# Expert products of a routed two-layer network interleaved on TensorE, with the second weight's two f16 parts side by side

## The chip, the cores and the metric

One core of one Trainium2 chip runs the whole kernel. The metric is the device time of one execution in microseconds; the time given for a kernel is the median of its runs. A profiled execution, which has its own time, gives the trace.

## The reference

```
x = x + attn(layernorm(x))       # gated linear recurrence, 32 sequences of 256 tokens, width 128
x = x + ffn(layernorm(x))

def ffn(x):
    h = layernorm(x) * g1 + be1
    x = x + softmax_attention(h) @ Wo             # 16 heads of 8
    m = layernorm(x) * g2 + be2                   # 8192 tokens x 128
    probs = softmax(m @ Wg)                       # 8 experts
    wts, idx = top_k(probs, 2); wts = wts / sum(wts)
    h1 = gelu(m @ W1[e] + b1[e])                  # 128 -> 512, tanh form
    ye = h1 @ W2[e] + b2[e]                       # 512 -> 128
    return x + sum over the two chosen e of wts[e] * ye
```

Only the two chosen experts of each token are computed. The change is in the last four lines, the expert stage.

## The kernel before, in words

The stages run one after another: norm and recurrence, projections, attention in two parts of 16 sequences, each followed by routing (the tokens of each expert are counted, and each token-expert pair gets a row in the DRAM buffer `expert_in`). Then comes the expert stage, then a gather of the two result rows of every token from `expert_out`, and the weighted sum.

**The expert stage** works on 80 blocks (`NBLK`) of 256 rows (`BS`), 40 for each part of the tokens. A block belongs to one expert, whose number stands in the table `blke`; each engine loads it into a register (`value_load`) and uses it to address the weights. Numbers are carried as two f16 parts, high and low, and a product is the sum of three: high by high, high by low, low by high. For each block:

- **Load** (SyncE, `load_block`, L439): a DMA that transposes the block's 256 rows of f16 pairs into `XT[q]`, one of four buffers, and raises `xt_in[q]`.
- **up** (TensorE): for each of four chunks of 128 hidden units, three products over 256 columns, 12 in all, into the PSUM banks 2 to 5. It waits for `xt_in` and for the gelu of two blocks before, which frees the banks.
- **gelu** (ScalarE, L834): four activations of 128x256 from PSUM to `G32` (two buffers), with the bias.
- **split** (VectorE): L1145 makes the high part `GH` in f16, L1147 the low part `GL`. Each has two buffers; a split waits until the down product two blocks before is done.
- **down** (TensorE): for each half of 128 rows and each of four chunks, three products over 128 columns, 24 in all, into bank 6 or 7. The gelu parts are the stationary operand, the weight parts `w2h`, `w2l` the moving one.
- **y_out** (VectorE, L1153): adds the bias of the expert (`b2s`, spread over all partitions) to the 128x256 result and writes `YB`; then `yb_ready` rises.
- **Store** (SyncE, `store_block`, L435): `YB` to `expert_out`.

All TensorE products are recorded on line L1191, that of the helper `mm`.

**The order** is set by each engine's program; `blocks` runs the first four blocks and the last eight straight, and those between in a loop with four blocks in its body. In iteration b TensorE does up(b+2), then down(b). VectorE does split(b+1), then y_out(b-1). ScalarE is two blocks ahead. SyncE's order is `blocks_io`: in iteration b it waits for `up_done` of block b (whose `XT` buffer the load takes), issues the load of block b+4, then waits for `yb_ready` of block b and issues its store. A load of block b+4 therefore stands in SyncE's queue behind the store of block b-1.

GpSimd scatters the rows of the second part into `expert_in` during the first 30 blocks (L620, paced by `down_done`), and gathers rows of the first part during the last 40 (L662, paced by `down_done` too); 64 gathers of the second part follow when all stores are done. During attention it splits the expert weights in `split_weight`; before the second sequence's `expand` it has nothing else of the expert stage.

```
for b in range(first, 4): body(b, b % 4)
with eng.Fori(r0, r1) as r:
    for q in range(4): body(4 * r + q, q)
for b in range(NBLK - 8, NBLK): body(b, b % 4)
```

Of the kernel before, what the change touches and what calls it, by code (L numbers as in the profile page):

```python
# [6 lines left out]
ALU = mybir.AluOpType  # L7
# [56 lines left out]
def layer_kernel(nc, x, w_hg, b_hg, w_out, b_out, h0, g1, be1, g2, be2, wq, wk, wv, wo, wg, w1, b1,  # L64
# [8 lines left out]
    with ctx:  # L73
        def sb(name, shape, dt=F32):
            return ctx.enter_context(nc.sbuf_tensor(name, shape, dt))

        def sem(name):
            return ctx.enter_context(nc.semaphore(name))
# [35 lines left out]
        wos = sb("wos", [P, D])  # L114
        wgs = sb("wgs", [P, NE])
        b1s = sb("b1s", [P, NE * FC])
        b2s = sb("b2s", [P, NE, D])
        wst = [sb(f"wst{s}", [P, F]) for s in range(2)]
        w1h, w1l, w2h, w2l = (sb(n, [P, NE, F], F16) for n in ("w1h", "w1l", "w2h", "w2l"))
# [33 lines left out]
        CN = view(2 * D).rearrange("p (t d) -> p t d", t=2)  # L153
        CNT = view(SL)

        at[0] = 0
        MT = [view(2 * 512) for _ in range(2)]

# [15 lines left out]
        GH = [view(FC * BS, F16) for _ in range(2)]  # L174
        GL = [view(FC * BS, F16) for _ in range(2)]
        YB = [view(2 * D).rearrange("p (h d) -> p h d", h=2) for _ in range(2)]

        at[0] = 0
# [8 lines left out]
        bout_in = sem("bout_in")  # L187
        params_in = sem("params_in")
        more_in = sem("more_in")
        x_in = [sem(f"x_in{k}") for k in range(NO)]  # L190
        dve_own = sem("dve_own")
        pool_own = sem("pool_own")
# [143 lines left out]
        def _(sp):  # L336
# [10 lines left out]
            def more(dst, src):  # L347
                sp.dma_start(dst, src).then_inc(more_in, 16)
# [23 lines left out]
            par(wgs[:, :], wg)  # L372
            more(blkn[:, :], const_blk)
            more(b1s[:, :], b1)
            more(b2s[:, :, :], b2.rearrange("(a e) d -> a e d", a=1).broadcast_to([P, NE, D]))

            sp.wait_ge(x_in[NO - 1], 16)
            sp.wait_ge(zero_ready, 1)
# [82 lines left out]
        def _(pool):  # L461
# [116 lines left out]
                    last.then_inc(va_ready, 1)  # L578

            def split_weight(k):  # L580
                whi, wlo = (w1h, w1l) if k < NE else (w2h, w2l)
                e, src = k % NE, wst[k % 2][:, :]
                pool.wait_ge(wst_in[k % 2], 16 * (k // 2 + 1))
# [4 lines left out]
                nc.gpsimd.tensor_copy(whi[:, e, :], src).then_inc(wsplit, 1)  # L588
                pool.wait_ge(wsplit, 2 * k + 1)
                nc.gpsimd.tensor_tensor(wlo[:, e, :], src, whi[:, e, :], ALU.subtract).then_inc(wsplit, 1)  # L590

            pool.wait_ge(rows_clear, 16 * (NBLK * BS // 512))
            expand(0)
            expand(1)
            for b in range(2, SEQ0[1]):
                expand(b)
                split_weight(b - 2)
# [249 lines left out]
        def _(dve):  # L847
# [159 lines left out]

            def b1_add(k):
                dve.wait_ge(b1_done, k + 1)
                dve.wait_ge(more_in, 48)  # L1010
# [61 lines left out]
            def route(part):  # L1072
# [12 lines left out]
                dve.wait_ge(more_in, 48)  # L1085
# [53 lines left out]

            def split(b, s):
                dve.wait_ge(gelu_done, b + 1)
                used(dve, down_done, b - 1)
                V.tensor_copy(GH[s], G32[s]).then_inc(gh_own, 1)  # L1145
                dve.wait_ge(gh_own, b + 1)
                V.tensor_tensor(GL[s], G32[s], GH[s], ALU.subtract).then_inc(gl_ready, 1)  # L1147

            def y_out(b, s):
                e = dve.value_load(blke[0:1, bass.ds(b, 1)], min_val=0, max_val=NE - 1)  # L1150
                dve.wait_ge(down_done, b + 1)
                used(dve, yb_out[s], 8 * (b - s))
                V.tensor_tensor(YB[s], bank[6 + s][:, 0:2 * D].rearrange("p (h d) -> p h d", d=D),  # L1153
                                b2s[:, bass.ds(e, 1), :].broadcast_to([P, 2, D]), ALU.add).then_inc(yb_ready, 1)

            def experts(b, q):
                if exists(b + 1):
                    split(b + 1, (q + 1) % 2)
                if exists(b - 1):
                    y_out(b - 1, (q + 1) % 2)  # L1160

            blocks(dve, -1, experts)
            y_out(NBLK - 1, 1)

# [23 lines left out]
        def _(pe):  # L1189
# [262 lines left out]
            pe.wait_ge(tab_ready, 2)  # L1452
            pe.wait_ge(wsplit, 4 * NE)

            def expert_of(b):
                return pe.value_load(blke[0:1, bass.ds(b, 1)], min_val=0, max_val=NE - 1)

            def part(w, e, c):
                return w[:, bass.ds(e, 1), P * c:P * c + P].rearrange("p a f -> p (a f)")

            def up(b, q):
                s = q % 2
                e = expert_of(b)
                pe.wait_ge(xt_in[q], 4 * (b - q) + 16)
                used(pe, gelu_done, b - 1)
                for c in range(FC):
                    dst = bank[2 + 2 * s + c // 2][:, BS * (c % 2):BS * (c % 2) + BS]
                    mm(dst, part(w1h, e, c), XT[q][:, 0, :], stop=False)
                    mm(dst, part(w1h, e, c), XT[q][:, 1, :], start=False, stop=False)
                    last = mm(dst, part(w1l, e, c), XT[q][:, 0, :], start=False)  # L1470
                last.then_inc(up_done, 1)

            def down(b, s):
                e = expert_of(b)
                pe.wait_ge(gl_ready, b + 1)
                used(pe, yb_ready, b - 1)
                for h in range(2):
                    dst = bank[6 + s][:, P * h:P * h + P]
# [5 lines left out]
                last.then_inc(down_done, 1)  # L1484

            def experts(b, q):
                if exists(b + 2):
                    up(b + 2, (q + 2) % 4)
                if exists(b):
                    down(b, q % 2)  # L1490

            blocks(pe, -2, experts)

# [38 lines left out]
```

## Time and profile before

| | us |
|---|---|
| median of three runs | 1227.25 |
| lowest, highest | 1223.43, 1246.7 |
| the profiled execution | 1236.04 |
| its span | 1234.2 |
| expert stage, first up product to last store's issue | 824.9 to 1139.6 |
| what follows (gathers, weighted sum, output) | 1139.6 to 1234.2 |
| TensorE, VectorE, ScalarE, GpSimd busy, whole span | 852.9, 834.6, 605.0, 471.1 |

Of the 1.84 us between the profiled time and its span nothing stands in the trace. Times in the trace count from the start of the span. An engine's row says when an instruction began and how long it took. "issue" means that the engine waited for nothing that the profile shows, which is the case when its own sequencer had not yet handed it the next instruction. A chain row says what the end of the kernel hung on at that time.

### The profile page before, as it was taken

All of it is one profiled execution on the core that took longest, in us unless ns stands there. A gap on an engine that the chain in (4) does not pass through costs nothing.

```text
span 1234.2 us, 27025 instructions
## 1 busy us (share of the span) xinstructions
PE 852.9 (69%) x8846; PEld 516.5 (42%) x8847; DVE 834.6 (68%) x1670; ACT 605.0 (49%) x1225; POOL 471.1 (38%) x548
## 2 busy tenths in 40 slices
PE   2577476688888884578888887448888888888000
PEld 1355344134443332513333333436666666666000
DVE  6778687768778846688888881845555555556622
ACT  3545288157677774227777775414444443333000
POOL 5800296002212123413333332735554045544774
PEclk9989799569999997559999997559999999999555
DMA  6900024211111110001111110013333233333422
GB/s 162 360 2 1 1 103 154 69 37 53 44 45 53 53 58 1 0 18 49 52 55 47 47 36 14 1 39 88 97 97 94 68 94 96 96 95 93 134 70 68
DMA packets 132213, 84.70 MB, mean 69 GB/s; under 512 B 54534, under 2 KB 117642, under 8 KB 132122
## 3 DMA queue, kind: packets, MB, share of 16 engines
q1 hardware_dynamic: 123930, 66.71, 18.7%
q0 software_dynamic: 8192, 16.79, 4.9%
q8 instruction: 55, 0.90, 0.3%
q14 instruction: 36, 0.29, 0.1%
HBM read 30.77 MB, written 41.94 MB: 59 GB/s over the span
## 4 chain that ended last, share of the span: by engine, by line
PE 52%; DVE 25%; issue 9%; POOL 7%; ACT 3%; DMA 2%; another core or an unknown queue 2%; DVEq 0%; SPq 0%; ACTq 0%; POOLq 0%
PE bank L1191 49%; DVE arena L1004 9%; POOL rr L466 2%; DVE arena L1147 2%; DVE mom L861 2%; DVE arena L940 2%; POOL Z L662 2%; POOL xh L470 2%; POOL HT L662 1%; DVE arena L1145 1%; PE bank L1371 1%; PE bank L1378 1%; DMA arena<-expert_in 1%; PE bank L1195 1%
## 5 line engine op out<-in xcount | busy, mean ns | idle before, releaser
L1004 DVE TENSOR_REDUCE arena<-bank 128x2 f32<-128x512 f32 x512 | 337.2, 688 | 85.0 <-PE bank L1191 82.9
L754 ACT ACTIVATE arena<-bank 128x512 f32<-128x512 f32 x512 | 292.8, 596 | 136.0 <-PE bank L1191 133.0
L1191 PE MATMUL bank<-QK 32*128 32x256 f16 (+1 forms) x2048 | 206.9, 288 | 91.3 <-DVE arena L1004 68.0
L620 POOL DMA_INDIRECT expert_in<-HT,idx x128 | 134.5, 1051 | 253.8 <-PE bank L1191 226.3
L834 ACT ACTIVATE arena<-bank,b1s 128x256 f32<-128x256 f32 x320 | 125.5, 476 | 179.6 <-PE bank L1191 120.1
L1191 PEld LDWEIGHTS bank<-QK 31*128 31x128 f16 (+1 forms) x2048 | 63.5, 93 | 241.6 <-ACT arena L754 177.6
L1191 PE MATMUL bank<-w2h,arena 128*128 x1280 | 143.0, 221 | 24.7 <-issue 15.7
L1191 PE MATMUL bank<-arena,VA 128*32 128x256 f32 x2048 | 145.7, 405 | 1.4 <-ACT arena L754 1.4
L1145 DVE CAST arena<-arena 128x1024 f16<-128x1024 f32 x80 | 55.5, 694 | 131.9 <-PE bank L1191 121.1
L1191 PE MATMUL bank<-arena,w1h 128*128 128x256 f16 x640 | 112.1, 277 | 33.9 <-issue 21.4
L1191 PEld LDWEIGHTS bank<-w2h,arena 128*128 128x128 f16 x1280 | 110.2, 96 | 52.1 <-issue 46.7
L1191 PE MATMUL bank<-w2l,arena 128*128 x640 | 122.7, 217 | 0.0
L1195 PE MATMUL bank<-cst,xh 128*128 128x128 f32 x192 | 44.9, 387 | 86.0 <-ACT xh L793 32.6
L662 POOL DMA_INDIRECT Z<-expert_out,idx x64 | 68.9, 1076 | 89.6 <-DMA expert_out<-arena 48.1
L466 POOL TENSOR_TENSOR rr<-vv,mhalf 128x8 f32<-128x8 f32 (+1 forms) x24 | 49.8, 2074 | 133.3 <-DVE vv L878 132.0
L1147 DVE TENSOR_TENSOR arena<-arena 128x1024 f16<-128x1024 f32 x80 | 98.1, 1226 | 2.7
L1191 PE MATMUL bank<-arena,w1l 128*128 128x256 f16 x320 | 88.4, 276 | 0.0
L662 POOL DMA_INDIRECT HT<-expert_out,idx x64 | 68.1, 1063 | 44.7 <-PE bank L1191 27.0
L1191 PEld LDWEIGHTS bank<-arena,w1h 128*128 x640 | 56.0, 99 | 54.5 <-issue 47.3
L1191 PEld LDWEIGHTS bank<-arena,VA 128*32 128x32 f32 x2048 | 55.2, 113 | 55.0 <-issue 25.2
L1195 PEld LDWEIGHTS bank<-cst,xh 128*128 128x128 f32 x192 | 31.3, 198 | 95.6 <-issue 49.5
L1191 PEld LDWEIGHTS bank<-w2l,arena 128*128 128x128 f16 x640 | 61.8, 96 | 0.8 <-issue 0.2
(148 smaller groups left out, 1213.5 us busy)
## 6 DMA issues: line engine op xcount, KB each, us to landing
QK<-qk_parts SPq DMA_DIRECT2D x96, 128.0 KB
expert_in<-arena SPq DMA_DIRECT2D x40, 256.0 KB, 3.6
expert_out<-arena SPq DMA_DIRECT2D x80, 128.0 KB
qk_parts<-arena SPq DMA_DIRECT2D x16, 512.0 KB, 2.8
X<-x SPq DMA_DIRECT2D x8, 512.0 KB, 5.9
wst<-w SPq DMA_DIRECT2D x16, 256.0 KB, 2.8
out<-arena SPq DMA_DIRECT2D x16, 256.0 KB
expert_in<-HT,idx POOLq DMA_INDIRECT x128, 2.2
```

Source lines behind the costliest of these rows:

```text
L466: nc.gpsimd.tensor_tensor(rr[j % 2][:, 0:n, :], vv[j % 2][:, 0:n, :], mhalf[:, 0:n, :], ALU.pow)\
L470: return nc.gpsimd.tensor_scalar(dst, src, rr[j % 2][:, n, t:t + 1], nmr[j % 2][:, n, t:t + 1], ALU.mult, ALU.add)
L620: pool.indirect_dma_start(xs, bass.IndirectOffsetOnAxis(idx[:, k, n:n + 1], 0), MHL[:, n, :], None).then_inc(scattered[n // HN], 16)
L662: pool.indirect_dma_start(gat[k][:, n, :], None, ys[0:BS * BLK0[part + 1], :], bass.IndirectOffsetOnAxis(idx[:, k, n:n + 1], 0))\
L754: nc.scalar.activation(PT[t % 8], bank[2 + t % 2][:, :], ACT.Exp, scale=DH ** -0.5)\
L834: last = nc.scalar.activation(G32[s][:, BS * c:BS * c + BS], bank[2 + 2 * s + c // 2][:, BS * (c % 2):BS * (c % 2) + BS], ACT.Gelu_apprx_t ...
L861: last = V.bn_stats(mom[:, t, :], buf[:, 8 * j + t, :])
L1004: V.tensor_reduce(nmax[n % 2][:, :, 4 * j + g], bank[u % 2][:, :].rearrange("p (q t) -> p q t", q=2), AX.X, ALU.max, negate=True).then_inc ...
L1145: V.tensor_copy(GH[s], G32[s]).then_inc(gh_own, 1)
L1147: V.tensor_tensor(GL[s], G32[s], GH[s], ALU.subtract).then_inc(gl_ready, 1)
L1191: return nc.tensor.matmul(dst, lhsT, rhs, start=start, stop=stop)
L1195: last = nc.tensor.transpose(bk[:, P * t:P * t + P], src[:, t0 + t, :], ident)
```

## The change

- TensorE: in iteration b it does up(b+3) and down(b), and their products alternate in the program: one of up, then one or two of down, twelve turns. All four waits (`xt_in`, `gelu_done`, `gl_ready`, `yb_ready`) stand ahead of the first product. The expert numbers are kept where they can be: seven loads of a number for four blocks in place of eight.
- down: the two parts of the second weight lie side by side in `w2p`, so that the high gelu part meets both in one product of 256 columns; the low gelu part meets the high weight in one of 128 columns. The output bias is one more product for each half, of `ones16` with `b2h`, whose rows 0 and 32 hold its two f16 parts. That is 8 products of 256 columns and 10 of 128 in place of 24 of 128. The result takes a whole bank, two partial sums side by side.
- VectorE: y_out becomes a reduction over the two partial sums (512 elements in, 256 out of each partition) and loads no expert number; in iteration b it does y_out(b-1) first, then split(b+2). `GH` and `GL` have four buffers, in the memory of `QK`.
- SyncE's order is as it was. The broadcast load of `b2s` (512 KB) becomes two loads of 4 KB. GpSimd makes `b2h` between expand(1) and expand(2): a memset, two copies and a subtraction.

```
 def split_weight(k):
-    whi, wlo = (w1h, w1l) if k < NE else (w2h, w2l)
+    if k < NE: whi, wlo = w1h[:, e, :], w1l[:, e, :]
+    else: ... whi, wlo = w2p[:, e, :, 0, :], w2p[:, e, :, 1, :]
...
+nc.gpsimd.memset(b2h[:, :, :], 0.0).then_inc(b2_own, 1)
+pool.wait_ge(more_in, 64)
+pool.wait_ge(b2_own, 1)
+for r in (0, 32):
+    nc.gpsimd.tensor_copy(b2h[r:r + 1, :, :], b2in[r:r + 1, :, :]).then_inc(b2_own, 1)
+pool.wait_ge(b2_own, 3)
+nc.gpsimd.tensor_tensor(b2h[32:33, :, :], b2in[32:33, :, :], b2h[32:33, :, :], ALU.subtract)
...
-def split(b, s):
+def split(b, q):
     dve.wait_ge(gelu_done, b + 1)
-    used(dve, down_done, b - 1)
+    used(dve, down_done, b - 3)
...
 def y_out(b, s):
-    e = dve.value_load(blke[0:1, bass.ds(b, 1)], min_val=0, max_val=NE - 1)
     dve.wait_ge(down_done, b + 1)
     used(dve, yb_out[s], 8 * (b - s))
-    V.tensor_tensor(YB[s], bank[6 + s][:, 0:2 * D]..., b2s[:, bass.ds(e, 1), :].broadcast_to([P, 2, D]), ALU.add)
+    V.tensor_reduce(YB[s], bank[6 + s][:, :].rearrange("p (h k d) -> p h d k", h=2, k=2), AX.X, ALU.add)
...
 def experts(b, q):                       # VectorE
-    if exists(b + 1): split(b + 1, (q + 1) % 2)
     if exists(b - 1): y_out(b - 1, (q + 1) % 2)
+    if exists(b + 2): split(b + 2, (q + 2) % 4)
...
 def down(b, q, e):                       # TensorE, a generator now, as up is
     for h in range(2):
         for c in range(FC):
-            mm(dst, GH[s][:, x], part(w2h, e, c), start=c == 0, stop=False)
-            mm(dst, GH[s][:, x], part(w2l, e, c), start=False, stop=False)
-            last = mm(dst, GL[s][:, x], part(w2h, e, c), start=False, stop=c == FC - 1)
+            w = w2p[:, bass.ds(e, 1), c, :, :].rearrange("p a k d -> p (a k d)")
+            mm(dst, GH[q][:, x], w, start=c == 0, stop=False)
+            yield
+            w = w2p[:, bass.ds(e, 1), c, 0, :].rearrange("p a d -> p (a d)")
+            mm(dst[:, 0:P], GL[q][:, x], w, start=False, stop=False)
+            yield
+        last = mm(dst[:, P:2 * P], ones16[:, :], b2h[:, bass.ds(e, 1), :]..., start=False)
...
 def experts(b, q):                       # TensorE
-    if exists(b + 2): up(b + 2, (q + 2) % 4)
-    if exists(b): down(b, q % 2)
+    u, qu = b + 3, (q + 3) % 4
+    if q == 0: known.clear()
+    for x, k in ((u, q + 3), (b, q)):
+        if exists(x) and k not in known: known[k] = expert_of(x)
+    if exists(u):
+        pe.wait_ge(xt_in[qu], 4 * (u - qu) + 16)
+        used(pe, gelu_done, u - 1)
+        ups = up(u, qu, known[q + 3])
+    if exists(b):
+        pe.wait_ge(gl_ready, b + 1)
+        used(pe, yb_ready, b - 1)
+        downs = down(b, q, known[q])
+    for turn in range(12):
+        for _ in zip(range(1), ups): pass
+        for _ in zip(range(1 + turn % 2), downs): pass
```

## Rows read from the trace of the kernel before

**Rows 1.** Engines by stretch: start:end, length, busy (instructions), granted clock, DMA share, GB/s.
```profile
220.00:260.00 40.00, 31.57 (x192) 8.41 (x196) 28.84 (x45) 12.65 (x22) 0.00 (x0) 0.50 0.16 46
...
844.00:884.00 40.00, 33.31 (x368) 26.66 (x366) 22.67 (x31) 15.70 (x40) 21.95 (x20) 1.00 0.39 100
```

**Rows 2.** Groups of instructions by form, 844 to 1130 us.
```profile
L1191 PE MATMUL bank<-w2h,arena 128*128 x1175 | 131.2, 221 | 22.4 <-issue 14.7 <-DVE arena L1147 6.2 <-DVE arena L1153 1.5
L834 ACT ACTIVATE arena<-bank,b1s 128x256 f32<-128x256 f32 x295 | 115.8, 475 | 171.9 <-PE bank L1191 113.2 <-issue 43.0 <-DVE arena L1147 15.7
...
L1191 PE MATMUL bank<-arena,w1h 128*128 128x256 f16 x592 | 101.6, 274 | 24.2 <-issue 21.4 <-DMA arena<-expert_in 1.2
...
L1147 DVE TENSOR_TENSOR arena<-arena 128x1024 f16<-128x1024 f32 x74 | 90.7, 1226 | 2.5
...
L1145 DVE CAST arena<-arena 128x1024 f16<-128x1024 f32 x73 | 50.7, 694 | 117.3 <-PE bank L1191 117.3
```

**Rows 3.** The chain that ended last, in order of time, expert stage: start, us, what.
```profile
822.01 2.71 DMA arena<-expert_in
824.93 2.75 PE bank L1191 x12
...
843.78 1.48 PE bank L1191 x12
...
904.52 1.79 PE bank L1191 x24
906.39 1.48 PE bank L1191 x12
...
1127.42 1.48 PE bank L1191 x12
```

**Rows 4.** Timeline of TensorE within one down product, both halves.
```profile
904.63 0.22 PE L1191 MATMUL bank<-w2l,arena 128*128 x1
...
904.87 0.22 PE L1191 MATMUL bank<-w2l,arena 128*128 x1
...
905.53 0.22 PE L1191 MATMUL bank<-w2l,arena 128*128 x1
...
905.70 0.22 PE L1191 MATMUL bank<-w2l,arena 128*128 x1
```

**Rows 5.** TensorE's sequencer, loads of an expert number: ns min/median/max, first and last start.
```profile
L1456 PEldq TENSOR_LOAD <-blke x147: 296/303/631, 844.7 to 1128.4; - x147
```

**Rows 6.** The chain that ended last, unmerged, 1108 to 1145 us.
```profile
1115.08 0.43 DVE arena L1153
...
1116.27 3.76 DMA arena<-expert_in
...
1120.16 1.48 PE bank L1191 x12
...
1137.18 1.87 PE bank L1191 x24
...
1139.18 0.43 DVE arena L1153
```

**Rows 7.** Timeline of SyncE's queue, blocks in the steady stretch.
```profile
893.30 0.38 SPq L435 DMA_DIRECT2D expert_out<-arena  x1
893.81 1.20 SPq L439 DMA_TRANSPOSE arena<-expert_in  x1
896.90 0.38 SPq L435 DMA_DIRECT2D expert_out<-arena  x1
897.91 1.20 SPq L439 DMA_TRANSPOSE arena<-expert_in  x1
```

**Rows 8.** Costliest groups of the page: a reduction of 512 PSUM elements on VectorE.
```profile
L1004 DVE TENSOR_REDUCE arena<-bank 128x2 f32<-128x512 f32 x512 | 337.2, 688 | 85.0 <-PE bank L1191 82.9
```

**Rows 9.** Timeline of GpSimd in attention, idle time in brackets.
```profile
261.63 0.53 POOL L576 COPY VA<-HT 128x128 f32<-128x128 f32 x2 [53.33 <-PE bank L1191]
```

More of the change, by code:

```diff
@@ L116, in layer_kernel @@
         b1s = sb("b1s", [P, NE * FC])
-        b2s = sb("b2s", [P, NE, D])
+        b2h = sb("b2h", [P, NE, D], F16)
         wst = [sb(f"wst{s}", [P, F]) for s in range(2)]
-        w1h, w1l, w2h, w2l = (sb(n, [P, NE, F], F16) for n in ("w1h", "w1l", "w2h", "w2l"))
+        w1h, w1l = (sb(n, [P, NE, F], F16) for n in ("w1h", "w1l"))
+        w2p = sb("w2p", [P, NE, FC, 2, D], F16)
         QK = [sb(f"QK{s}", [P, 4, 2, SL], F16) for s in range(4)]
@@ L154, in layer_kernel @@
         CNT = view(SL)
+        at[0] = 5472
+        b2in = view(NE * D).rearrange("p (e d) -> p e d", d=D)
         at[0] = 0
@@ L173, in layer_kernel @@
         G32 = [view(FC * BS) for _ in range(2)]
-        GH = [view(FC * BS, F16) for _ in range(2)]
-        GL = [view(FC * BS, F16) for _ in range(2)]
+        GH, GL = ([QK[s][:, 2 * k:2 * k + 2, :, :].rearrange("p a b t -> p (a b t)") for s in range(4)]
+                  for k in range(2))
         YB = [view(2 * D).rearrange("p (h d) -> p h d", h=2) for _ in range(2)]
@@ L580, in split_weight @@
             def split_weight(k):
-                whi, wlo = (w1h, w1l) if k < NE else (w2h, w2l)
                 e, src = k % NE, wst[k % 2][:, :]
+                if k < NE:
+                    whi, wlo = w1h[:, e, :], w1l[:, e, :]
+                else:
+                    src = src.rearrange("p (c d) -> p c d", d=D)
+                    whi, wlo = w2p[:, e, :, 0, :], w2p[:, e, :, 1, :]
                 pool.wait_ge(wst_in[k % 2], 16 * (k // 2 + 1))
@@ L1453, in _, with up_part, up @@
             pe.wait_ge(wsplit, 4 * NE)
+            pe.wait_ge(b2_ready, 1)
             def expert_of(b):
                 return pe.value_load(blke[0:1, bass.ds(b, 1)], min_val=0, max_val=NE - 1)
-            def part(w, e, c):
+            def up_part(w, e, c):
                 return w[:, bass.ds(e, 1), P * c:P * c + P].rearrange("p a f -> p (a f)")
[L1461 to L1465, printed above, removed]
-                for c in range(FC):
[L1467 to L1470, printed above, removed]
+            def up(b, q, e):
+                for c in range(FC):
+                    dst = bank[2 + 2 * (q % 2) + c // 2][:, BS * (c % 2):BS * (c % 2) + BS]
+                    mm(dst, up_part(w1h, e, c), XT[q][:, 0, :], stop=False)
+                    yield
+                    mm(dst, up_part(w1h, e, c), XT[q][:, 1, :], start=False, stop=False)
+                    yield
+                    last = mm(dst, up_part(w1l, e, c), XT[q][:, 0, :], start=False)
+                    if c < FC - 1:
+                        yield
@@ L1471, in up, with down @@
                 last.then_inc(up_done, 1)
[L1473 to L1476, printed above, removed]
+                yield
+            def down(b, q, e):
                 for h in range(2):
-                    dst = bank[6 + s][:, P * h:P * h + P]
+                    dst = bank[6 + q % 2][:, 2 * P * h:2 * P * h + 2 * P]
                     for c in range(FC):
                         x = slice(BS * c + P * h, BS * c + P * h + P)
-                        mm(dst, GH[s][:, x], part(w2h, e, c), start=c == 0, stop=False)
-                        mm(dst, GH[s][:, x], part(w2l, e, c), start=False, stop=False)
-                        last = mm(dst, GL[s][:, x], part(w2h, e, c), start=False, stop=c == FC - 1)
+                        w = w2p[:, bass.ds(e, 1), c, :, :].rearrange("p a k d -> p (a k d)")
+                        mm(dst, GH[q][:, x], w, start=c == 0, stop=False)
+                        yield
+                        w = w2p[:, bass.ds(e, 1), c, 0, :].rearrange("p a d -> p (a d)")
+                        mm(dst[:, 0:P], GL[q][:, x], w, start=False, stop=False)
+                        yield
+                    last = mm(dst[:, P:2 * P], ones16[:, :], b2h[:, bass.ds(e, 1), :].rearrange("p a d -> p (a d)"),
+                              start=False)
+                    if h == 0:
+                        yield
@@ L1484, in down @@
                 last.then_inc(down_done, 1)
+                yield
+            known = {}
             def experts(b, q):
-                if exists(b + 2):
-                    up(b + 2, (q + 2) % 4)
-                if exists(b):
-                    down(b, q % 2)
-            blocks(pe, -2, experts)
+                u, qu = b + 3, (q + 3) % 4
+                if q == 0:
+                    known.clear()
+                for x, k in ((u, q + 3), (b, q)):
+                    if exists(x) and k not in known:
+                        known[k] = expert_of(x)
+                ups, downs = [], []
+                if exists(u):
+                    pe.wait_ge(xt_in[qu], 4 * (u - qu) + 16)
+                    used(pe, gelu_done, u - 1)
+                    ups = up(u, qu, known[q + 3])
+                if exists(b):
+                    pe.wait_ge(gl_ready, b + 1)
+                    used(pe, yb_ready, b - 1)
+                    downs = down(b, q, known[q])
+                for turn in range(12):
+                    for _ in zip(range(1), ups):
+                        pass
+                    for _ in zip(range(1 + turn % 2), downs):
+                        pass
@@ L1496 @@
+            blocks(pe, -3, experts)
 def kernel(**inputs):
```

29 lines of the change are left out of this document (17 added, 12 removed).

## The prediction

>
> Inside a period an up product takes 1.48 us for 12 instructions [rows 3]; the last needs 0.27 of it (274 ns, rows 2), so one starts every 0.11. In a down product three start in 0.24 us in the first half and in 0.17 in the second [rows 4]: 0.080 and 0.057 each. Both halves have the same shapes. What differs is that the second uses weight addresses that the first has already worked out. So where addresses are new the sequencer sets the pace: 12 products with 8 addresses take 0.96 us, 0.12 for an address. Starts sum to 12 x 0.11 + 12 x 0.080 + 12 x 0.057 = 2.96 us; the other 0.87 of the period are the gaps ahead of up and down, where the sequencer loads an expert number (0.30 us median, up to 0.63 [rows 5], plus the arithmetic around it; I take 0.7 in all) and waits for semaphores. The bound now is TensorE's sequencer, serial: two numbers, 16 addresses, four waits.
>
> **TensorE's own work after.** Products: 12 + 8 of 256 columns, 8 + 2 of 128. By the starts above 20 x 0.11 + 10 x 0.057 = 2.77 us against 12 x 0.11 + 24 x 0.057 = 2.69 at the same pace, so the array has 0.08 us more to do. From first start to last end it is 2.77 - 0.06 + 0.22 = 2.93, which I call M. The sequencer loses three addresses (8 for up, 4 for down, 1 for the bias, if both slices of `w2p` at chunk c, which begin at one address, share it) and a quarter of a number: 3.83 - 0.36 - 0.17 = 3.30 us. The pure gain of interleaving would therefore be 0.5 us a block, 39 us over 74. That is what I don't expect to see, because of the next part.
>
> **The load of XT comes onto the path.** Up now runs three blocks ahead, but SyncE's order is unchanged. The load of block b+4 is queued behind the store of b-1, which waits for y_out(b-1), which waits for the end of down(b-1). Before, up(b+4) stood in iteration b+2, two periods (7.7 us) after that end. Now it stands in iteration b+1, and its wait stands ahead of all 30 products, so down(b+1) waits too. The loop: start of iteration b-1, M, y_out, store issue, load, start of iteration b+1. That is 2P = M + L. L, step by step:
> - end of down to start of y_out: 1139.05 to 1139.18, 0.13 [rows 6].
> - y_out: 128x512 from PSUM. The nearest row is another reduction of 512 PSUM elements, 0.69 us [rows 8]. It writes 2 elements, this one 256. Below it can't be less than the 0.43 of the present y_out [rows 6]; above I put twice the row, 1.38. I take 0.69.
> - end of y_out to issue of the load: 1115.51 to 1116.27, 0.76 [rows 6]. In the steady stretch the load follows the start of the store by 0.51 us, and by 1.01 once in four, where the loop wraps [rows 7]. Over four it is some 0.70, and 0.17 before the store gives 0.87. Ends: 0.70 and 1.2.
> - issue to landing: 2.71 with nothing else moving [rows 3], 3.76 beside gathers [rows 6]. No row shows a plain one in the middle; a scatter runs beside it there. I take 2.6, near the lower row, for bounds of 2.2 and 3.76.
> - landing to first product: 1120.03 to 1120.16, 0.13 [rows 6], and two more waits behind `xt_in` (for the split and for y_out), which before stood elsewhere, at an estimated 0.1 each: 0.33.
>
> L = 0.13 + 0.69 + 0.87 + 2.6 + 0.33 = 4.62, and P = (2.93 + 4.62) / 2 = 3.78. The blocks of one parity carry the wrap and the pair goes by the slower, so 3.80.
>
> **The other loops.** VectorE does split(b+3) between y_out(b) and y_out(b+1). Up(b+3) ends 2.7 us into iteration b, gelu takes up to 4 x 0.475 = 1.9, the split 0.69 + 1.23 [rows 2], hand-overs 0.2: done at 6.7. Y_out(b+1) is due at P + M + 0.13 = 6.86. So it is in time with 0.1 to spare, and as a loop over three periods (6.7 + 0.69 + 0.87 + 2.6 + 0.33 = 11.2) it asks for 3.73 only. VectorE's work is 0.69 + 1.23 + 0.69 = 2.6 of 3.80. ScalarE's is unchanged. Four `GH` and `GL` buffers remove a wait that cost little.
>
> **Start and tail.** The first blocks hang on gelu(0) to (2) and the stores as before; up(5) still needs the load behind the store of block 0, so I take no gain there. After up(79) begins, the old kernel needed 12.2 us to the last store (1127.42 to 1139.6). The new one has M = 2.9 with down(76), three downs at 1.45 of products and 0.5 of gap, and y_out 0.8: 9.6, say 10. Gain 2.2. The gathers behind the last store are untouched.
>
> **GpSimd's bias preparation** falls into 53.3 us of idle time ahead of the third `expand` [rows 9]; four instructions, the larger of 1024 elements on one partition, an estimated 6 us at most. Nothing, and 6 us if that cover were gone. The smaller bias DMA ends long before its first use: nothing either way.
>
> **Sum.** 74 x (3.83 - 3.80) = 2.2, and 2.2 of the tail: 4.4 us less than the profiled 1236.04, so 1231.6. The shown median is 1227.25, 0.7% below the profiled one; at the same ratio the changed kernel comes to 1222.8. I forecast 1222.
>
> **Two rules weighed.** Rows 4 show down products starting 0.057 us apart, each with a new 128-column stationary operand. The Trainium skill (TensorE: Matmul & The Clock Gate, "LDWEIGHTS (loading the stationary operand)") gives a load the operand's columns over 1.2, an estimated 107 ns here; taken as serial work that would be 36 x 0.107 = 3.85 us before and 30 x 0.107 = 3.21 after, 46 us faster. By that rule; the trace disagrees, since 24 such products took 1.79 us [rows 3].
>
> The first of rows 1 is a stretch ahead of the steady part of attention, with TensorE busy 31.6 of 40 us at a granted clock of 0.50, the 1.2 GHz level. So a busy engine alone does not guarantee the clock, and after the change the array stands still some 0.9 us in 3.8, for a transfer. The same page of the Trainium skill ("Loop structure matters more than you think") calls a DMA wait between groups of products bad for the clock. By that rule the change would be slower; in the trace the old loop has 0.87 us of gaps at 1.00.
>
> **The rivals.**
> - *Faster, the load is cheaper than I think.* With 2.2 for the landing, 0.70 for SyncE and 0.25 after it, 2P = 2.93 + 0.13 + 0.69 + 0.70 + 2.2 + 0.25 = 6.90, P = 3.45: 28 + 2 us less, 1197. For it: the DMA engines are busy only 0.39 of the time [rows 1]. Against: both landings in the rows are above 2.7.
> - *Slower, the same loop at its upper prices.* The alternating reduction at 1.1 and the landing at 3.2, as beside gathers: 2P = 8.56, P = 4.28: 33 - 2 us more, 1258. The loop decides for slower from 2P = 7.73 on, for slower by 2% from 8.4. For it: the 3.76 row, and gathers run beside the second 40 blocks. Against: only a few loads show it.
> - *Addresses not shared* (17 instead of 13). The sequencer needs 3.78, and the first half of the products is paced by it, M = 3.13: P = 3.90, 5 - 2 us more, 1230.
> - *The clock falls.* Twelve up products took 2.75 at the low clock against 1.48 [rows 3]; M doubles to 5.8, P = 5.2, some 100 us more, 1327.
> - *Weight loads bound* as by the page: 1181.
>
> **Chances.** Forecast 0.60, cheaper load 0.13, dearer load 0.13, addresses 0.09, clock 0.03, weight loads 0.02. A measurement of this kernel tells about 2% from no change. Faster: 0.13 + 0.02 = 0.15; slower: 0.13 + 0.03 = 0.16; the rest, 0.69, within. The forecast's own spread (landing 2.4 to 2.9) is 1212 to 1236; the range runs toward the two load cases, 1197 to 1250.
>
> **What the profile would show.** TensorE's idle time put down to the load of `arena` from `expert_in` or to "issue" right behind it, some 0.8 us once per block; 30 products as one run of 2.9 us; y_out at 0.69, its store and then the load about 0.9 behind its end; the period 3.80. It is wrong if TensorE waits for nothing and the period is near 3.4, if the wait is for the split, or if y_out takes over 1 us.

## The result and the profile after

The changed kernel took 1232.9 us against 1226.1 (medians of 18 runs each); the ratio is 1.0047, 95% interval 1.0025 to 1.0070. The forecast was 1222. Two later comparisons of the same kernel gave 0.9995 (0.9967 to 1.0023) and 1.0029 (1.0003 to 1.0055), so it is even or a few tenths of a per cent slower, and not faster by the 0.4% of the forecast. The profiled execution took 1232.73 us, span 1230.9. All ratios leave out the executions that took over 1.5% more than the fastest of their kernel; where such a long one is the profiled one, as with two blocks behind, its extra time lies ahead of the expert stage.

Who waited for whom, changed kernel, 850 to 1130 us (engine, line, releaser: us in total, times, longest):

```profile
DVE QK L1165 <- ACT arena L854: 57.3, 71, 1.0
PE bank L1209 <- DMA arena<-expert_in: 55.1, 58, 2.2
...
PE bank L1209 <- ACT arena L854: 12.6, 7, 2.0
```

TensorE's wait for the load of `XT` was 1.2 us before, in the row of the up products [rows 2]. It is 55.1 now, at 58 places, and the "issue" that stood beside it in rows 2 (14.7 and 21.4 us) is no longer among TensorE's waits. VectorE's split waited 117.3 us behind TensorE [rows 2] and now waits 57.3 for the gelu. The last row, TensorE behind the gelu, belongs to the load as well. The program asks there only for the gelu of up(b+1), which ended long before. At the first block of a loop body the products begin 0.45 us after the load has landed, and where a later gelu ends within that time the row names it: products begin at 911.63 us, their load landed at 911.18, a gelu ended at 911.51. Each of the seven has its load landed 0.13 to 0.50 us ahead. The chain says the same where it passes through the load, and carries the loop link by link. The chain that ended last, changed kernel:

```profile
836.55 2.94 PE bank L1209 x30
...
958.08 2.95 PE bank L1209 x30
...
961.14 0.70 DVE arena L1172
...
962.61 2.65 DMA arena<-expert_in
...
965.40 2.94 PE bank L1209 x30
...
1131.80 2.95 PE bank L1209 x30
```

Thirty products in 2.95 us, 0.11 to the reduction, 0.70 for it, 0.77 to the issue of the load (962.61 less 961.84), 2.65 to its landing, 0.14 to the next 30: 7.32 us. Those next 30 are two iterations on, since the iteration between hangs on the load before. This loop is one of the short ones. The mean of the 56 between 870 and 1090 us is 7.77, which is 3.88 a block. SyncE's queue in the changed kernel (L442 is the store, L446 the load):

```profile
899.72 0.38 SPq L442 DMA_DIRECT2D expert_out<-arena  x1
...
900.31 1.20 SPq L446 DMA_TRANSPOSE arena<-expert_in  x1
...
910.84 0.38 SPq L442 DMA_DIRECT2D expert_out<-arena  x1
911.86 1.20 SPq L446 DMA_TRANSPOSE arena<-expert_in  x1
```

The load follows the start of the store by 0.59 us, and by 1.02 where the loop wraps; it was 0.51 and 1.01 before [rows 7].

For the period, the first and last y_out of a stretch and their count serve best. The row of y_out in the changed kernel and in the kernel before, 870 to 1096 us (ns min/median/max, first and last start):

```profile
L1172 DVE TENSOR_REDUCE arena<-bank x58: 680/691/693, 871.2 to 1093.1; 128x256 f32<-128x512 f32 x58
```

```profile
L1153 DVE TENSOR_TENSOR arena<-bank,b2s x58: 416/417/418, 873.3 to 1095.2; 128x256 f32<-128x256 f32 x58
```

Both are 221.9 us over 57 steps, 3.893 us a block. This part of the stage did not move at all. In these two profiles the difference lies outside it. Stretches of the changed kernel (length, busy TensorE, weight loads, VectorE, ScalarE, GpSimd, granted clock, DMA share, GB/s); the two of 3.4 us were chosen after the clock's own record:

```profile
844.00:884.00 40.00, 29.39 (x271) 24.62 (x271) 22.95 (x27) 13.67 (x36) 17.24 (x18) 0.91 0.33 88
884.00:924.00 40.00, 30.50 (x313) 26.23 (x314) 26.07 (x32) 16.72 (x43) 19.04 (x20) 1.00 0.37 97
...
1084.00:1120.00 36.00, 27.37 (x252) 22.87 (x250) 20.96 (x25) 12.56 (x32) 13.34 (x13) 0.91 0.35 87
...
846.80:850.20 3.40, 3.40 (x22) 2.59 (x20) 0.00 (x0) 0.06 (x1) 0.00 (x0) 0.51 0.00 0
...
1116.50:1119.90 3.40, 3.40 (x21) 2.62 (x19) 0.64 (x1) 0.00 (x0) 0.00 (x0) 0.50 0.17 38
```

In four spells (from 846.8, 863.9, 1099.4 and 1116.5) the clock was granted at 0.50, the 1.2 GHz level, with TensorE busy throughout and 22 products in such a stretch. Some 1 us before each spell a standstill of 2.0 us or more had ended. Two of these waits, timeline of TensorE, idle time in brackets:

```profile
845.71 0.28 PE L1209 MATMUL bank<-arena,w1h 128*128 128x256 f16 x1 [2.85 <-DMA arena<-expert_in]
...
1098.32 0.28 PE L1209 MATMUL bank<-arena,w1h 128*128 128x256 f16 x1 [2.21 <-DMA arena<-expert_in]
```

TensorE in the kernel before never stood for 1.6 us in this stage once down had begun. The sum of the stage, after against before: first product to up(5) 15.7 against 18.8 us (-3.2); up(5) to up(79) 295.25 against 287.23 (+8.0, the spells' part); up(79) to the last store 10.2 against 8.6 (+1.6). Together that is +6.4 us. It is close to the 6.8 us between the medians, but it doesn't explain them: of these two profiled executions the changed kernel's is the shorter one, by 3.3 us, since what lies outside the stage was 9.7 us shorter in it. Nor do the first and second term stay the same from one profile to the next, as the table at the end of the experiments shows.

### The profile page after: what moved, and what is told of

Read it like the earlier page. It is cut to its first block, busy times and chain, and to the rows that moved or that the text cites. A ratio compares the mean times of both kernels' runs of the same rounds, so it can differ in the third digit from the quotient of the medians.

```text
span 1230.9 us, 25465 instructions
## 1 busy us (share of the span) xinstructions
PE 826.3 (67%) x8366; PEld 510.8 (41%) x8367; DVE 860.6 (70%) x1669; ACT 604.6 (49%) x1225; POOL 453.4 (37%) x552
## 4 chain that ended last, share of the span: by engine, by line
PE 44%; DVE 23%; POOL 9%; DMA 9%; issue 8%; ACT 4%; SPq 1%; ACTq 0%; DVEq 0%; POOLq 0%
PE bank L1209 41%; DVE arena L1024 9%; DMA arena<-expert_in 8%; POOL Z L682 2%; POOL HT L682 2%; POOL rr L473 2%; DVE arena L1172 2%; DVE mom L881 2%; POOL xh L477 2%; DVE arena L960 2%; PE bank L1389 1%; SPq L442 1%; ACT arena L854 1%; PE bank L1396 1%; PE bank L1213 1%
## 5 line engine op out<-in xcount | busy, mean ns | idle before, releaser
L1209 PE MATMUL bank<-arena,w1h 128*128 128x256 f16 x640 | 170.9, 282 | 84.0 <-DMA arena<-expert_in 68.6
L640 POOL DMA_INDIRECT expert_in<-HT,idx x128 | 124.8, 975 | 266.7 <-PE bank L1209 239.2
L1209 PE MATMUL bank<-w2p,QK 128*128 x1280 | 221.6, 250 | 1.6 <-DVE arena L1172 1.6
L1209 PEld LDWEIGHTS bank<-w2p,QK 128*128 128x128 f16 x1280 | 126.0, 99 | 14.2 <-issue 1.7
L1209 PEld LDWEIGHTS bank<-arena,w1h 128*128 x640 | 64.2, 101 | 103.1 <-issue 96.8
L1165 DVE CAST QK<-arena 128x1024 f16<-128x1024 f32 x80 | 55.6, 696 | 70.4 <-ACT arena L854 70.4
L1167 DVE TENSOR_TENSOR QK<-arena,QK 128x1024 f16<-128x1024 f32 x80 | 98.0, 1226 | 2.7
L682 POOL DMA_INDIRECT Z<-expert_out,idx x64 | 61.9, 967 | 100.7 <-PE bank L1209 82.5
L1172 DVE TENSOR_REDUCE arena<-bank 128x256 f32<-128x512 f32 x80 | 55.0, 689 | 44.1 <-PE bank L1209 42.2
L583 POOL COPY VA<-HT 128x128 f32<-128x128 f32 x64 | 16.8, 297 | 100.9 <-PE bank L1209 100.9
```

The lines of the kernel that those rows point to most:

```text
L640: pool.indirect_dma_start(xs, bass.IndirectOffsetOnAxis(idx[:, k, n:n + 1], 0), MHL[:, n, :], None).then_inc(scattered[n // HN], 16)
L682: pool.indirect_dma_start(gat[k][:, n, :], None, ys[0:BS * BLK0[part + 1], :], bass.IndirectOffsetOnAxis(idx[:, k, n:n + 1], 0))\
L1165: V.tensor_copy(GH[q], G32[q % 2]).then_inc(gh_own, 1)
L1167: V.tensor_tensor(GL[q], G32[q % 2], GH[q], ALU.subtract).then_inc(gl_ready, 1)
L1172: V.tensor_reduce(YB[s], bank[6 + s][:, :].rearrange("p (h k d) -> p h d k", h=2, k=2), AX.X, ALU.add) .then_inc(yb_ready, 1)
L1209: return nc.tensor.matmul(dst, lhsT, rhs, start=start, stop=stop)
```

## The experiments

Each comparison is with the kernel before, run on the same chip; ratios carry a 95% interval. The period is worked out as above from the row of y_out, over 870 to 1080 us.

**Load issued ahead.** The changed kernel with SyncE's order altered (block 4's load is issued ahead of the loop, after the first up product):

```
-                if exists(b + 4):
-                    sp.wait_ge(up_done, b + 1)
-                    load_block(b + 4, q)
+                if exists(b + 5):
+                    sp.wait_ge(up_done, b + 2)
+                    load_block(b + 5, (q + 1) % 4)
                 store_block(b, q % 2)
```

> The changed kernel with one edit on SyncE: the load of block b+5 is issued ahead of the store of block b, so a load no longer stands behind the store of the block before last. Theory (the load of XT came onto the path; behind it the sequencer of TensorE, 3.30 us a block, or gelu and split set the pace): TensorE's wait for that load goes, the period falls from 3.99 to 3.3 to 3.5 us, the granted clock stays at 1.00 in the expert stage, and the time is 1185 to 1205. Rival (products alternating, or the reduction on VectorE, make the block slow, and the load is only what ends last): at most 5 us less, 1228 to 1233.

Measured 0.9693 (0.9654 to 0.9733), 1202.9 us on a chip where the kernel before took 1236.9. Rows of the up products and of y_out, this run:

```profile
L1211 PE MATMUL bank<-arena,w1h 128*128 128x256 f16 x496 | 130.0, 273 | 31.5 <-DVE QK L1169 24.6 <-issue 6.9
```

```profile
L1174 DVE TENSOR_REDUCE arena<-bank x62: 683/689/693, 871.4 to 1079.2; 128x256 f32<-128x512 f32 x62
```

The wait for the load is gone, a wait for the split (L1169) has taken a part of its place, and the period is 207.8 / 61 = 3.41. (The 3.99 of the expectation is 295.25 / 74, with the spells in it.) Moving one load in SyncE's program is worth 3.5% here: the load was the bound.

**The same order in the kernel before.**

> The kernel before with the same edit on SyncE. Theory: it has two periods for a load and its own sequencer bounds it, so nothing moves: 1222 to 1230. Rival (loads queued behind stores cost time there too): 5 to 30 us less.

Measured 0.998 (0.995 to 1.001), period 3.89. Nothing moved, so the old kernel has no load on its path, and the change put it there.

**Two blocks behind instead of three**, products alternating.

```
-                u, qu = b + 3, (q + 3) % 4
+                u, qu = b + 2, (q + 2) % 4
```

> The changed kernel with down two blocks behind up instead of three (products alternating all the same, VectorE splits block b+1 in iteration b, six numbers loaded for four blocks, SyncE as it was). Theory: the load has a period more and leaves the path; next is the loop up, gelu, split, down over two blocks, about 6.8 us, so 3.4 a block: 1185 to 1200. Rival (alternating products are slow themselves): 1228 or more. Rival (split on the path costs more than three blocks of distance would): 3.8 or more a block, 1222 and above.

Measured 0.9767 (0.9734 to 0.9801), period 3.57. The load has left the path. The chain of this run shows what took it over:

```profile
934.58 2.88 PE bank L1209 x28
...
938.74 0.49 ACT arena L854
939.34 0.69 DVE QK L1165
940.07 1.24 DVE QK L1167
...
941.65 2.93 PE bank L1209 x30
```

From one run of products over gelu and split to the next but one, 7.07 us for two blocks. The loop was foreseen at 6.8: the place was right, and the price 0.3 us too low.

**The new shape alone**, in the old order and not alternating:

```
+            def experts(b, q):
+                if exists(b + 2):
+                    e = expert_of(b + 2)
+                    ...
+                    for _ in up(b + 2, (q + 2) % 4, e): pass
+                if exists(b):
+                    e = expert_of(b)
+                    ...
+                    for _ in down(b, q, e): pass
```

> The kernel before in its order (up two ahead, then down, not alternating; eight numbers for four blocks), with the second weight's parts side by side, the bias by TensorE and the reduction on VectorE. Theory (the sequencer bounds the block; three addresses of 0.12 us go): 3.83 - 0.36 = 3.47 us a block, 1196 to 1206. Rival (the array bounds it, and has 0.08 us a block more to do): 1230 to 1234.

Measured 0.9724 (0.9662 to 0.9787), 1201.95 us. y_out in this run:

```profile
L1172 DVE TENSOR_REDUCE arena<-bank x61: 683/684/685, 871.8 to 1079.3; 128x256 f32<-128x512 f32 x61
```

```profile
L1209 PEldq FUSED_REGOPS  x549: 46/46/46, 870.4 to 1079.5; - x183
...
L1209 PEldq ALU_OP  x244: 32/32/36, 870.5 to 1078.1; - x122
```

That is 793 in 61 blocks, 13 a block. The kernel before has 432 and 432 in 54 blocks, 16 a block, and the changed kernel 13 again.

**Four addresses put back.** On that kernel, `w2p[..., c, 0, :]` for the low gelu part becomes `w2p[..., c, 1, :]`: this leaves out the product of the low gelu part with the high weight and makes one with the low weight instead, of the same shape, from another address.

> The kernel of the run with the new shape alone, but the low gelu part meets the low half of the second weight instead of the high one, so that part of the product is another number than the reference's; the shapes and counts are the same, but each chunk has two weight addresses instead of one, four more for a block. Theory (0.12 us of sequencer for an address): 0.48 us a block more, 3.9, so 33 to 38 us above that run, a ratio of 0.995 to 1.005 to the kernel before. Rival (addresses are hidden behind products): under 8 us more.

Measured 1.008 (1.005 to 1.011).

```profile
L1172 DVE TENSOR_REDUCE arena<-bank x52: 676/684/684, 872.9 to 1078.7; 128x256 f32<-128x512 f32 x52
```

205.8 / 51 = 4.04: 0.58 us for four addresses, 0.144 each, the same price from the other side. The count of register instructions is 889 in 52 blocks, 17 a block.

**Fewer numbers.** The new shape alone, with the number of up(b+2) kept for down where both stand in one body of the loop (`known[q + 2] = expert_of(b + 2)`).

> The kernel of the run with the new shape alone (up two ahead, not alternating), and the number of an expert loaded for up is kept for down where both stand in one loop body: six loads of a number for four blocks in place of eight. Theory (TensorE's sequencer sets the period, a number costs it 0.7 us): half a load a block less, 0.35 us of 3.45, so some 24 us less than that run, a ratio of 0.95 to 0.96 to the kernel before, unless the loop of gelu and split (about 3.3 a block) ends the gain at half. Rival (the array or VectorE sets the period there): no change, 0.97.

Measured 0.9629 (0.9577 to 0.968), 1185.95 us, period 206.8 / 63 = 3.28. A gain of 0.18, half of the 0.35 of half a number. The expectation had that figure as its second case, but with another cause: TensorE's waits for gelu and split come to 4.8 us between 870 and 1090 us, and its up products waited 8.9 us for loads.

**Both.** That kernel with the load issued ahead.

> The fastest kernel so far (new shape, products not alternating, six numbers for four blocks) with the load of block b+5 ahead of the store of block b. Theory: its own profile still shows a little waiting for loads, some 9 us in the steady 220 us; most of that goes, 3 to 8 us less, a ratio of 0.956 to 0.961 to the kernel before. Rival (the loop of gelu and split takes it over): no change, 0.963.

Measured 0.9597 (0.9527 to 0.9668), 1174.65 us: the fastest of all, ahead of both kernels by 4%.

```profile
L1174 DVE TENSOR_REDUCE arena<-bank x67: 682/683/685, 870.7 to 1079.3; 128x256 f32<-128x512 f32 x67
```

Period 208.6 / 66 = 3.16. The intervals of this run and the one before overlap; the step between them is not settled by the times, but the period fell by 0.12.

**The fastest kernel, alternating.** Two behind, six numbers, load ahead, products alternating and all waits ahead of them. VectorE's order differs too: it sums before it splits.

> The fastest kernel (two behind, six numbers, load ahead) with its products alternating and all waits ahead of them, as in the changed kernel; VectorE sums before it splits. Theory: alternating gives the sequencer nothing it did not have, and now up waits for the split of the block that down needs: the loop up, gelu, split, down of two blocks stays at 3.5 us a block, as in the run two behind: a ratio of 0.970 to 0.980 to the kernel before, some 20 us slower than the fastest. Rival (alternating hides addresses and numbers behind longer products): 3.19 or less, 0.96 or less.

Measured 0.9851 (0.9803 to 0.9899), period 208.9 / 59 = 3.54, against 3.16 without alternating. It is slower than expected by 0.005, but on the side of the theory. Between 870 and 1080 us TensorE waited 13.6 us for the split and 12.3 us for y_out, ahead of up products that need neither. What alternating, the place of the waits and VectorE's order cost by themselves was not separated. The period is also that of the run with two blocks behind (3.57), which has the old order of loads: there the load had indeed left the path.

**A dearer step in the loop, first.** Each store as two DMAs of 128 rows.

> The changed kernel with each store issued as two DMAs of 128 rows instead of one of 256, so that the load behind it is issued about 0.45 us later. Theory (period is half of M + L): 0.22 us a block more, some 17 us more than the changed kernel, a ratio of 1.015 to 1.022 to the kernel before, more if the clock falls oftener. Rival (the load is not on the path): no change, 1.005. Rival (the wait is one period long, not two): 0.45 a block, 33 us, 1.03.

Measured 1.0107 (1.0074 to 1.014), below the expected 1.015 to 1.022. SyncE's queue and then the chain of this run:

```profile
899.69 0.86 SPq L443 DMA_DIRECT2D expert_out<-arena  x2
900.79 1.20 SPq L446 DMA_TRANSPOSE arena<-expert_in  x1
```

```profile
897.00 2.67 DMA arena<-expert_in
899.80 2.94 PE bank L1209 x30
902.76 0.70 DVE arena L1172
904.82 2.69 DMA arena<-expert_in
907.64 2.94 PE bank L1209 x30
```

The load is issued 1.10 us after the start of the store instead of 0.59, and this loop is 7.84 us from one run of products to the next but one.

**The second, on VectorE.** The reduction done twice, first into an unused tile.

```
+                V.tensor_reduce(YD[s], bank[6 + s][:, :].rearrange("p (h k d) -> p h d k", h=2, k=2), AX.X, ALU.add)
                 V.tensor_reduce(YB[s], bank[6 + s][:, :].rearrange("p (h k d) -> p h d k", h=2, k=2), AX.X, ALU.add)
```

> The changed kernel with each reduction of VectorE done twice, first into an unused tile: 0.73 us more between the end of down and the store. Theory (the period is half of M + L): 0.36 us a block more, 27 us, a ratio of 1.024 to 1.030 to the kernel before, and the split stays beside it, since VectorE is then at 3.3 us a block. Rival (the load is not on the path): 1.005. Rival (the wait returns every block): 0.73 a block, 54 us, 1.049.

Measured 1.0184 (1.0112 to 1.0255), below the expected 1.024 to 1.030.

Between 1041 and 1080 us this profile has four spells at half the clock, and the run before has one at 1040.2. So the period is compared ahead of them. Rows of y_out, 870 to 1035 us, in the changed kernel, with the store in two and with the reduction twice:

```profile
L1172 DVE TENSOR_REDUCE arena<-bank x43: 680/691/693, 871.2 to 1033.7; 128x256 f32<-128x512 f32 x43
```

```profile
L1172 DVE TENSOR_REDUCE arena<-bank x42: 684/692/693, 871.0 to 1034.0; 128x256 f32<-128x512 f32 x42
```

```profile
L1174 DVE TENSOR_REDUCE arena<-bank x41: 678/680/682, 872.3 to 1032.1; 128x256 f32<-128x512 f32 x41
```

The periods are 3.87, 3.98 and 4.00. From the end of down to the issue of the load the two runs take 0.47 and 0.59 us more than the changed kernel, in the mean of the loops that begin between 870 and 1030 us, and the block grew by 0.11 and 0.13. Both runs reject a price of nothing and one that returns every block. Half of what was added, the price by M + L, is 0.23 and 0.30, and they fall short of that too: in the same loops the landing and the step from it to the products are together 0.29 and 0.32 us shorter than in the changed kernel. With that the loops add up, as the parts of a loop must; it is no test of the theory, and why the landing is shorter is not known. It isn't that slower loops have shorter landings. The medians of the loads issued between 870 and 1090 us, read from the events of their semaphores, are 2.57 us in the kernel before (period 3.89), 2.90, 2.75 and 2.60 in the three profiles of the changed kernel, 2.57 with its load ahead (3.41), and 2.81 in the fastest kernel (3.16). In the third profile of the changed kernel a quarter of the landings is not recorded.

**The changed kernel again, and fillers.** Eight products of 128 columns into an unused bank ahead of the waits. Four runs: fillers, the kernel as it is, and then both side by side on one chip.

```
+                if exists(u) and exists(b):
+                    for _ in range(8):
+                        mm(bank[0][:, 0:P], ones16[:, :], ones16[:, :])
```

> The changed kernel with eight products of 128 columns into an unused bank ahead of the waits of each iteration, 0.46 us of array work inside the 0.5 to 1.3 us in which TensorE waits for the load. Theory (four spells at half the clock in the expert stage cost the profiled run about 7 us, and the load loop alone comes out even with the kernel before): the granted clock stays at 1.00 there, the period is 3.89, and the time is 4 to 8 us less than the changed kernel's, a ratio of 0.997 to 1.001 to the kernel before. Rival (the 6 us come from the loop itself): the ratio stays at 1.005 or rises, since the shorter gaps grow.

> The changed kernel as it is, beside the run with the doubled reduction and on the same chip. Theory: in the expert stage the granted clock falls again for a few short spells, not at the same blocks, since the stage stands still for the load each block; ratio to the kernel before 1.002 to 1.008. Rival (the four spells of the first profile were chance): 1.00 throughout and a ratio of 1.000.

> The changed kernel as it is, on the same chip and beside the run with fillers that follows. Theory (spells at half the clock are what puts it above the kernel before): its ratio lies above that of the run with fillers by 0.002 to 0.005, and runs with a lower mean clock are the longer ones. Rival (spells make no difference that can be measured): the two ratios agree within 0.001.

> The changed kernel with eight filler products ahead of the waits, again, beside the changed kernel. Theory: no or one spell at half the clock in the expert stage, and a ratio of 0.997 to 1.000 to the kernel before. Rival (fillers lengthen the short gaps as much as they save): the ratio is at or above the changed kernel's.

Fillers gave 1.0005 (0.9979 to 1.0031) and 0.9992 (0.9969 to 1.0014); the kernel as it is 0.9995 (0.9967 to 1.0023) and 1.0029 (1.0003 to 1.0055). So the second comparison of the kernel as it is met its rival, no spell and a ratio of 1.000, and not the theory; and fillers did not keep every spell away, the first run with them has one (a granted clock of 0.96 between 844 and 884 us). Side by side the difference is 0.0037, as the theory has it, but the intervals overlap. In the changed kernel the executions with a lower mean clock are indeed the longer ones, by some 9 us for 0.01 of clock, but so are those of the kernel before, by some 8, though its profile has no spell in this stage. So that part of the expectation came true without telling for the spells. Stretches of the second profile of the kernel as it is, and of the side-by-side pair (without and with fillers):

```profile
844.00:884.00 40.00, 28.07 (x290) 24.03 (x288) 24.82 (x30) 15.70 (x40) 17.60 (x19) 1.00 0.37 91
...
1084.00:1120.00 36.00, 28.12 (x292) 24.22 (x289) 24.59 (x29) 14.40 (x37) 16.36 (x16) 1.00 0.39 99
```

```profile
884.00:1084.00 200.00, 152.15 (x1547) 130.46 (x1547) 132.68 (x156) 80.87 (x207) 71.88 (x74) 0.99 0.35 91
```

```profile
884.00:1084.00 200.00, 178.83 (x1975) 153.80 (x1975) 133.93 (x157) 81.21 (x209) 71.27 (x75) 1.00 0.36 92
```

The expert stage in seven profiles (us; a spell is a stretch at half the clock, counted after the first 20 us):

| | first product to up(5) | up(5) to up(79) | up(79) to last store | spells |
|---|---|---|---|---|
| kernel before | 18.8 | 287.2 | 8.6 | 0 |
| kernel before, load ahead | 17.4 | 287.4 | 8.6 | 0 |
| changed kernel | 15.7 | 295.3 | 10.2 | 4 |
| changed kernel, second | 15.8 | 287.0 | 10.2 | 0 |
| changed kernel, third | 18.4 | 288.3 | 10.1 | 1 |
| with fillers | 15.7 | 290.0 | 10.1 | 1 |
| with fillers, second | 18.1 | 287.2 | 10.1 | 0 |

In the profile without a spell up(5) to up(79) took 286.96 us, where the one with four needed 295.25: 8.3 us, some 2 for each spell. That is shown, and that the rest of the loop is even with the kernel before. The last column but one is 1.5 us longer in every profile of the changed kernel. The first column differs as much between executions of one kernel as between the kernels. That spells make up what the first comparison has above 1.000 is possible and not shown, since times and spells were recorded together in only five executions.

## Why the prediction was wrong

- **The bound before** was named rightly: the sequencer, with its addresses and numbers. An address was put at 0.12 us; two runs measured 0.144 and 0.145 in the period.
- **One row was read wrongly.** The up product at 1127.42 is up(78), not up(79); the last stands inside the next chain row and began at 1131.01. Over 74 blocks the period before was 287.23 / 74 = 3.88, not 3.83, and the old tail 8.6 us, not 12.2. The two errors cancel in the sum, but they hid that the new tail, 10.2 us (10 was forecast), is longer than the old one.
- **The load comes onto the path:** right, with 2P = M + L. Means of the 56 loops that begin between 870 and 1090 us: M was put at 2.93 and is 2.93; end of down to the reduction 0.13 and 0.13; the reduction 0.69 and 0.69; SyncE 0.87 and 0.86; landing to first product 0.33 and 0.26 (0.13 in half of them, 0.45 at the first block of each loop body).
- **The step that failed** is the landing in L, "issue to landing: I take 2.6". It is 2.90 in the mean and in the median of these loops. So L is 4.84 and not 4.62, and P = (2.93 + 4.84) / 2 = 3.88 and not 3.78. Against the true base the forecast of 3.80 would have been a gain of 0.08 us in each of 74 blocks, 6 us; the measured period in the steady part is that of before. In the second profile the landing is 2.82 in the mean and the loop 7.72; in the third the loop is 7.78, with a spell in it and its landings recorded in part. The choice was near what the same load took in the kernel before, 2.57 in the median, which stood in no row. The forecast's own spread, 1212 to 1236, has the landing at up to 2.9, so the size was allowed for and the wrong value chosen. Why it lands later in the changed kernel stays open.
- **The tail** was the other half of the forecast gain and has the wrong sign: 2.2 us were to be won, and 1.5 were lost in every profile.
- **The clock** was a rival with all or nothing: half speed in every block, 100 us, 0.03. What came is in between: a few spells, four in the first profile, 8 us. The page of the Trainium skill that warns of a long wait for a DMA ahead of products (TensorE: Matmul & The Clock Gate, "Loop structure matters more than you think") pointed the right way, and the trace agrees with it: the waits of 2.0 us and more ahead of the four spells. The sentence set against it, that the old loop had 0.87 us of gaps at a clock of 1.00, compared short gaps with longer ones. A wait of 2.45 and one of 2.37 us in the second profile were followed by no spell, nor was one of 3.00 in the third, so a long wait does not bring one every time. The spell in the first run with fillers followed a standstill of 1.43 us only.
- **Start:** "I take no gain there" is not refuted. First product to up(5) took 15.7 us (820.89 to 836.55) in place of 18.8 (824.93 to 843.78), but 18.4 in the third profile of the changed kernel, and 17.4 in the kernel before with its load ahead.
- **GpSimd's preparation and the smaller bias DMA** left no trace in the waits of the expert stage; they were not tried alone.
- The rival "addresses not shared" is out: they are shared, since TensorE's sequencer works out 13 a block, and 17 in the run that made them differ, which cost 0.58 us a block.

## What to carry to other kernels

When a product is moved ahead, list every queue that feeds it and ask what stands before its load there: here the load stood behind the store of an older block, and moving up by one block without moving the load by one turned a gain of 3 to 4% into nothing. Count what a sequencer does serially (addresses, numbers, waits) before counting columns: fewer distinct weight addresses gave 0.43 us a block. The fastest kernel lost 0.38 us a block when its products alternated behind all the waits, with VectorE's order changed too, since that joins loops that had been apart. Where a forecast is made of a two-period loop, its result moves by half of any term, so the least known term, here the landing of a DMA, wants its own rows in the same surroundings, and more than one profile. A releaser named in a row of waits is checked against the program: a gelu that the program did not wait for stood there in place of the load. And a difference between two profiles is not laid to the change before a second profile of the same kernel has it too.

## What the runs showed of the hardware

- The landing of the same transposing load of 256 rows had a median of 2.57 us in the kernel before, and of 2.90, 2.75 and 2.60 in three profiles of the changed kernel; single ones took 2.3 to 3.7. What sets it was not found. Runs that put 0.47 and 0.59 us more into the loop found it some 0.25 us shorter.
- TensorE fell to half its clock for a short spell some 1 us after waits of 2.0 to 2.9 us, though it was busy when the clock fell and all through the spell. The same waits in another execution were followed by none.
- A product whose weight address depends on a register lengthened the block by about 0.144 us for each address that the sequencer had not worked out before, in two loops that it bounds; a 128-column product with a known address starts every 0.057 us [rows 4].
